# One weight product per rotated piece, and five fp4 pieces rounded by comparisons on VectorE and GpSimd and summed on TensorE

## What is computed

```python
# layer 0 attention: 16 heads of 32 for q, 8 for k and v, causal, soft cap 50
q, k = x @ Wq, x @ Wk                       # x: layernorm of the input
q = q * cos + rotate_half(q) * sin          # rotate_half: (-second half, first half) of each head's 32
k = k * cos + rotate_half(k) * sin
w = softmax(50 * tanh(q @ k.T / sqrt(32) / 50))   # masked
x = x + (w @ (x @ Wv)) @ Wo

# layer 0 feed-forward: weights rounded to fp4 in blocks of 32 along their input side
exp = floor(log2(max(max|w| over the block, 1e-30))) - 2
idx = digitize(|w / 2**exp|, [0.25, 0.75, 1.25, 1.75, 2.5, 3.5, 5.0])
w4  = sign(w) * [0, 0.5, 1, 1.5, 2, 3, 4, 6][idx] * 2**exp
```

## Time and profile before

| | |
|---|---|
| median of 3 runs | 1392.82 us (1390.68 to 1394.52) |
| the profiled execution | 1394.05 us, its span 1392.3 us |
| granted TensorE clock over the span | 0.953 |
| TensorE busy | 1239.9 us, 89% |
| VectorE busy | 817.3 us, 59% |
| ScalarE busy | 526.3 us, 38% |
| GpSimd busy | 329.8 us, 24% |

### The profile page before, as it was taken

One profiled execution on the slowest core, in us unless ns is written; L12 is line 12 of the kernel. 1 busy time (PEld: TensorE's weight loads), 2 busy tenths in 40 slices (PEclk: granted clock), 3 DMA queues, 4 the chain that ended last, 5 costly groups with the idle time before them and its releaser, 6 DMA issues. The chain is left out here.

```text
span 1392.3 us, 23432 instructions
## 1 busy us (share of the span) xinstructions
PE 1239.9 (89%) x9322; PEld 744.2 (53%) x9334; DVE 817.3 (59%) x2109; ACT 526.3 (38%) x967; POOL 329.8 (24%) x364
## 2 busy tenths in 40 slices
PE   5678779788999899899998998999999999994898
PEld 2246554456854544556664544555555555663455
DVE  2887767757687344768766766343111126777955
ACT  1019335563524433544444545111111114445453
POOL 0225502100003100245542221232222223450200
PEclk9688899998999999999999999999999999996999
DMA  9000000000040030000000000123232210000000
GB/s 384 1 0 3 1 1 2 0 1 1 1 197 2 10 112 1 1 2 3 3 2 1 2 2 1 52 75 95 80 106 80 84 37 1 2 3 0 1 1 31
DMA packets 13340, 48.02 MB, mean 34 GB/s; under 512 B 1688, under 2 KB 4888, under 8 KB 12464
## 3 DMA queue, kind: packets, MB, share of 16 engines
q1 hardware_dynamic: 13232, 46.53, 10.0%
HBM read 45.37 MB, written 1.15 MB: 33 GB/s over the span
## 5 line engine op out<-in xcount | busy, mean ns | idle before, releaser
L821 ACT ACTIVATE PT<-PS 128x384 f32<-128x384 f32 (+1 forms) x320 | 153.2, 531 | 189.3 <-PE PS L631 138.4
L1930 PE MATMUL PS<-HT,WA 128*128 128x512 f32 x448 | 201.5, 593 | 2.4 <-DVE MO L2008 2.0
L2008 DVE TENSOR_TENSOR MO<-PS,AO 128x512 f32<-128x512 f32 x56 | 38.7, 690 | 205.9 <-ACT AO L1998 205.8
L1930 PEld LDWEIGHTS PS<-HT,WA 128*128 128x128 f32 x448 | 84.7, 190 | 87.7 <-issue 82.9
L1998 ACT ACTIVATE AO<-PS 128x512 f32<-128x512 f32 x56 | 33.3, 597 | 247.9 <-PE PS L1930 247.9
L757 DVE CUSTOM_DVE_ANT_0 junk<-PS,TRI 128x128 bf16<-128x128 f32 (+1 forms) x384 | 112.6, 352 | 4.0 <-PE PS L612 0.2
L1938 PE MATMUL PS<-WA,HO 128*128 128x256 f32 x448 | 105.6, 378 | 0.0
L1938 PEld LDWEIGHTS PS<-WA,HO 128*128 128x128 f32 x448 | 84.5, 189 | 34.7 <-issue 24.9
L240 PE MATMUL PS<-identb 128*128 128x512 bf16 x388 | 99.2, 394 | 3.2 <-PEq L584 1.2
L2063 POOL TENSOR_TENSOR HO<-MO,GR 128x512 f32<-128x512 f32 x44 | 57.8, 1314 | 168.7 <-PE PS L1938 168.7
L612 PE MATMUL PS<-KS,QM 32*128 32x128 f32 (+1 forms) x768 | 86.7, 347 | 7.5 <-DVE QM L791 6.6
(11 more groups left out here) (323 smaller groups left out, 2412.8 us busy)
## 6 DMA issues: line engine op xcount, KB each, us to landing
WA<-w2f_in SPq DMA_DIRECT2D x28, 384.0 KB, 4.5
WA<-wl_in SPq DMA_DIRECT2D x1, 5137.0 KB, 16.0
GR<-gate_rows SPq DMA_DIRECT2D x20, 256.0 KB, 3.9
GB<-gate_rows SPq DMA_DIRECT2D x8, 512.0 KB, 7.4
WA<-wa_in SPq DMA_DIRECT2D x2, 1792.0 KB, 12.2
WB<-wb_in SPq DMA_DIRECT2D x1, 3208.0 KB, 18.4
WA<-wa_in SPq DMA_DIRECT2D x1, 2560.0 KB, 16.9
GR<-gate_rows SPq DMA_DIRECT2D x4, 448.0 KB, 4.0
```

Source lines behind the costliest of these rows:

```text
L821: act.activation(PT[:, g % 3, st_slot(k), 0:W], PS[:, st_bank(g, k), 0:W], ACT.Exp, scale=scale).then_inc(S["at_exp"], 1)
L1930: last = pe.matmul(PS[:, 2 * c + half, :], chunk(i, half)[:, k * P:(k + 1) * P], HT[:, k, c * CH:(c + 1) * CH], start=k == 0, stop=k == KD ...
```

## The change

It has four parts.

1. The swapped copies of the weights are gone, from the host's layout and from `a_in`. An item is a single product. VectorE exchanges the halves of each head by a stream shuffle from PSUM into `RS`, then multiplies the product by cos into `RC`. GpSimd multiplies `RS` by sin in place and adds. Four PSUM banks and four buffers now hold four items.
2. TensorE makes the product of v for tile n-2 right behind item n, in place of after all items. The context is turned behind the last item, in banks 4 and 5. GpSimd's wait for `b_in` is at the end of its block, and it waits for `const_in` first.
3. The five early pieces are rounded in another way. VectorE takes the largest of each block for all five pieces (items 1 to 3) and makes powers and inverses once on 80 columns. Per piece ScalarE makes the absolute value, VectorE scales it, and seven independent comparisons write 0 or a weight in bf16 into `IND`: four on VectorE, three on GpSimd. TensorE sums the seven by seven products with the bf16 identity (`identb`) into PSUM bank 6 or 7. VectorE joins sign and power (`SP`) and multiplies the sum by it. The pieces begin at the items 4, 5, 7, 8 and 10 (`turn`), TensorE sums two items later, or at the last item.
4. Beside the attention the same 51 steps now stand on 11 of the first 15 quads: none on the fourth quad of a batch, and none on the last.

```diff
-        work = [(w["q"], w["qp"], QT, j, c) for j in range(nq) for c in range(NCH)]
-        work += [(w["k"], w["kp"], KT, j, c) for j in range(2) for c in range(NCH)]
+        BUF = 4
+        work = [(w["q"], QT, j, c) for j in range(nq) for c in range(NCH)]
+        work += [(w["k"], KT, j, c) for j in range(2) for c in range(NCH)]
...
                 def _(pe):
-                    for n, (a, ap, _, j, c) in enumerate(work):
-                        if n >= 2:
-                            pe.wait_ge(S["rope_sin"], d["rope_sin"] + n - 1)
+                    for n, (a, _, j, c) in enumerate(work):
+                        if n >= 4:
+                            pe.wait_ge(S["rope_pair"], d["rope_pair"] + n - 3)
+                            pe.wait_ge(S["rope_cos"], d["rope_cos"] + n - 3)
+                        for k in range(KD):
+                            last = pe.matmul(PS[:, n % 4, :], a[:, k, j * P:(j + 1) * P],
+                                             HT[:, k, c * CH:(c + 1) * CH], start=k == 0, stop=k == KD - 1)
+                        last.then_inc(S["proj"], 1)
+                        t = n - 2
+                        if 0 <= t < TT:
...
+                        kernels["tensor"](pe, n, NW)
...
                 def _(dve):
+                        if n >= BUF:
+                            dve.wait_ge(S["rope_sum"], d["rope_sum"] + n - BUF + 1)
+                        dve.stream_shuffle(RS[:, n % BUF], ps, PAIR[hd]).then_inc(S["rope_pair"], 1)
+                        dve.tensor_tensor(wide(RC[:, n % BUF]), wide(ps), cos.to_broadcast([P, nchunk, T]),
+                                          ALU.mult).then_inc(S["rope_cos"], 1)
+                        kernels["vector"](dve, n, NW)
...
                 def _(pool):
+                    pool.wait_ge(S["const_in"], 16)
+                    for n, (_, dst, j, c) in enumerate(work):
+                        pool.wait_ge(S["rope_pair"], d["rope_pair"] + n + 1)
+                        pool.tensor_tensor(wide(RS[:, n % BUF]), wide(RS[:, n % BUF]), sin.to_broadcast([P, nchunk, T]),
+                                           ALU.mult).then_inc(S["rope_sin"], 1)
+                        pool.wait_ge(S["rope_sin"], d["rope_sin"] + n + 1)
+                        pool.wait_ge(S["rope_cos"], d["rope_cos"] + n + 1)
+                        pool.tensor_tensor(dst[:, j, c * CH:(c + 1) * CH], RC[:, n % BUF], RS[:, n % BUF], ALU.add).then_inc(S["rope_sum"], 1)
+                        kernels["beside"](pool, n, NW)
 
                     pool.wait_ge(S["b_in"], 64)
...
+        STEPS = [(5.0, 2.0), (3.5, 1.0), (2.5, 1.0), (1.75, 0.5), (1.25, 0.5), (0.75, 0.5), (0.25, 0.5)]
+        OWN = 4
...
+        def scaled(dve, m):
+            dve.wait_ge(S["q_sizes"], m + 1)
+            v = grp(at["scaled"][:, m % 4])
+            dve.tensor_tensor(v, v, wide(per(2, m)), ALU.mult).then_inc(S["q_scaled"], 1)
+        def sizes(act, m):
+            if m >= 4:
+                act.wait_ge(S["q_steps"], OWN * (m - 3))
+                act.wait_ge(S["q_steps_beside"], (len(STEPS) - OWN) * (m - 3))
+            act.activation(at["scaled"][:, m % 4], piece(m), ACT.Abs).then_inc(S["q_sizes"], 1)
+        def signed(dve, m):
+            if m >= 2:
+                dve.wait_ge(S["q_kept"], m - 1)
+            dve.scalar_tensor_tensor(u32(grp(at["signed"][:, m % 2])), u32(grp(piece(m))), 0x80000000, u32(wide(per(1, m))), ALU.bitwise_and,
+                                     ALU.bitwise_or).then_inc(S["q_signed"], 1)
+        def steps_of(eng, m, lo, hi, name):
+            eng.wait_ge(S["q_scaled"], m + 1)
+            if m >= 2:
+                eng.wait_ge(S["q_summed"], m - 1)
+            for j in range(lo, hi):
+                eng.tensor_scalar(at["steps"][:, m % 2, j, :], at["scaled"][:, m % 4], STEPS[j][0], STEPS[j][1], ALU.is_ge, ALU.mult).then_inc(S[name], 1)
+        def summed(pe, m):
+            for j in range(len(STEPS)):
+                last = pe.matmul(PS[:, 6 + m % 2, :], identb[:], at["steps"][:, m % 2, j, :], start=j == 0, stop=j == len(STEPS) - 1)
+            last.then_inc(S["q_summed"], 1)
+        def kept(dve, m):
+            dve.tensor_tensor(piece(m), PS[:, 6 + m % 2, :], at["signed"][:, m % 2], ALU.mult).then_inc(S["q_kept"], 1)
+        turn = {4: 0, 5: 1, 7: 2, 8: 3, 10: 4}
+        begun = {m: n for n, m in turn.items()}
...
         def beside_attention(dve, i, n):
-            lo, hi = (early * NS + (NP - early) * NS * min(j, n - 2) // (n - 2) for j in (i, i + 1))
+            lo, hi = (early * NS + (NP - early) * NS * min(j - j // 4, n - n // 4 - 1) // (n - n // 4 - 1) for j in (i, i + 1))
```

More of the change, by code:

```diff
@@ L892, in shifted_attention, with project @@
                 done[name] += k
-    def project(w, nq, hd, QT, KT, V, arrived=None, first=None, beside=None):
+    def project(w, nq, hd, QT, KT, V, kernels, arrived, first):
         cos = cst(f"cos{hd}", 1)
@@ L1126, in self_attention @@
         V = st.enter_context(nc.sbuf_tensor(f"V{layer}", [P, TT, D], F32))
-        project(w, nq, hd, QT, KT, V, arrived, first=masks, beside=beside[0])
+        project(w, nq, hd, QT, KT, V, beside[0], arrived, first=masks)
         copies, kernels = turn_kernels()
@@ new lines, in powers @@
+        def powers(dve):
+            a, b, c = (at["small"][:, j, :] for j in range(3))
+            dve.wait_ge(S["q_largest"], early)
+            dve.tensor_scalar(a, a, 1e-30, None, ALU.max).then_inc(S["q_powers"], 1)
+            dve.wait_ge(S["q_powers"], 1)
+            dve.tensor_scalar(u32(b), u32(a), 0x7F800000, None, ALU.bitwise_and).then_inc(S["q_powers"], 1)
+            dve.wait_ge(S["q_powers"], 2)
+            dve.tensor_scalar(b, b, 0.25, None, ALU.mult).then_inc(S["q_powers"], 1)
+            dve.wait_ge(S["q_powers"], 3)
+            dve.reciprocal(c, b).then_inc(S["q_powers"], 1)
+            dve.wait_ge(S["q_powers"], 4)
@@ new lines, in quantise_fp4, with beside_tensor, beside_vector @@
+        turn = {4: 0, 5: 1, 7: 2, 8: 3, 10: 4}
+        begun = {m: n for n, m in turn.items()}
+        def beside_tensor(pe, n, last):
+            for m in range(early):
+                if min(begun[m] + 2, last - 1) == n:
+                    summed(pe, m)
+        def beside_vector(dve, n, last):
+            if n in (1, 2, 3):
+                for m in range(2 * (n - 1), min(2 * n, early)):
+                    largest(dve, m)
+            if n == 3:
+                powers(dve)
+            if n in turn:
+                m = turn[n]
+                scaled(dve, m)
+                steps_of(dve, m, 0, OWN, "q_steps")
+            for m in range(early):
+                if begun[m] + 1 == n:
+                    signed(dve, m)
+                if begun[m] + 2 == n:
+                    kept(dve, m)
+            if n == last - 1:
+                kept(dve, early - 1)
@@ L2496, in gqa @@
         wk, wv = wk[:, cols], wv[:, cols]
-    if hd < 32:
-        return [blocks(a) for a in (wq, wk, wv, wo)]
-    return [blocks(a) for a in (wq, swapped(wq, hd, paired), wk, swapped(wk, hd, paired), wv, wo)]
+    return [blocks(a) for a in (wq, wk, wv, wo)]
 def layout(i):
```

137 lines of the change are left out of this document (66 added, 71 removed).

## The result

The changed kernel takes 1382.28 us (median of 6 runs, 1381.59 to 1383.8), the kernel before, run beside it, 1395.38 (1390.68 to 1400.27). The ratio is 0.9909, with an interval of 0.9893 to 0.9925: faster, by 13 us where 26 were forecast. The time lies above the range (1356 to 1379).

The account below looks back on a forecast made before the run. VectorE, busy for 61.85 of 67 us, was taken to bound the projection. The block ending 29 us earlier and the attention taking 3 more gave -26 us: 1368 from the profiled 1394.05, 1367 as median, range 1356 to 1379.

Parts of the forecast that it names:

- GpSimd's comparison: Projection: 15 comparisons new on GpSimd, priced at 0.77 us each from L2425, 11.6 us.
- GpSimd's lane: Projection: from 18.3 us, 42.1 of instructions, 6 of disturbance and 6.6 of waits, ending at 73.0.
- disturbance by VectorE: Projection: GpSimd loses 1.2 us per piece to VectorE's contested steps, 6 us in all.
- waits for a shuffle: Projection: GpSimd waits 1.65 us for the next item's shuffle at four of five pieces, 6.6 us.
- The last sum: End of projection: TensorE's last sum, 1.5 us or 3 at the low clock, hides behind GpSimd's last rotation.
- the whole walk: Projection: VectorE's and GpSimd's orders walked against each other; lanes end at 72.5 and 73.0, first attention product at 73.3.
- Rival B: Projection: GpSimd compares slower than it adds constants, 1.27 to 1.58 us each, +7 to +12, 1374 to 1379; 17%.
- rival E: Projection: slower than before, as GpSimd's comparison is too dear; decides at 2.5 us each, at 3.0 1400; 3%.
- The handing of work to GpSimd: Projection: three comparisons per piece on GpSimd; VectorE waits 3.9 us per piece in contested steps, 19 us.
- Rival C: Projection: TensorE at the low clock becomes the bound, 35 us of work become 70, 1382 us; 5%.
- rival F: Projection: VectorE and GpSimd exclude each other for whole instruction lengths, 1.32 in place of 1.05 us, 1370; 15%.
- The attention: Attention block: denser steps delay the first inversion 1.5 us and the second batch another 1.5; +3 us, between -2 and +6.

## Why the prediction was wrong in size and right in sign

**GpSimd's comparison** is the step that failed. It was priced at 0.77 us by a multiplication with an addition in the earlier trace rows, the nearest shape but another operation. The lane, term by term:

| GpSimd's lane, us | forecast | measured |
|---|---|---|
| first multiplication | 18.3 | 18.65 |
| 24 instructions with two inputs, undisturbed | 30.5 | 28.3 (12 x 1.09 + 12 x 1.27) |
| 15 comparisons, undisturbed | 11.6 | 28.8 (15 x 1.92) |
| disturbance by VectorE | 6 | 2.3 (0.5 + 0.6 + 1.2 of the three kinds) |
| waits for a shuffle | 6.6 | 1.8 |
| small gaps | 0 | 1.4 |
| end of its last rotation | 73.0 | 81.3 |
| then to the first attention product | 0.3 | 2.0 |

The comparisons give +17.2; the waits and disturbances shrink by 8.5, since VectorE now has time to be ahead; multiplication by sin in place is 2.2 cheaper in all, gaps and a later start cost 1.8: +8.3. The last sum, which was to hide behind the last rotation, adds 1.7. Near the assumed price the whole walk is right to 2.4 us, as the kernel with multiplication and addition shows, though there a disturbance that is too large by 2.8 makes up for waits that are too small by 2.7.

**Rival B** was the right mechanism, at 17%, but its own range ended at 1.58 us and 1379. The rows bounded it with instructions of other operations, and nothing in them excluded more; rival E even named the point (2.5 us) at which the price would make the kernel slower. With 1.92 in place of 0.77 the forecast's sum gives +17, 1384; the result is 1382.3. The upper bound was taken from the lengths of the nearest rows, although none of them was this comparison.

**The handing of work to GpSimd** was forecast to make VectorE wait for 19 us, and no kernel without it was among the rivals. With all seven on VectorE the block is 13 us shorter than in the changed kernel. It is 1.6 us shorter even than with GpSimd's instruction at 0.68 us (51.5 against 53.1 from GpSimd's first multiplication, the latter in one profile), so the handing over did not pay at the forecast's price either.

**TensorE** was not the bound: all five sums waited, for 1.5 to 7.7 us (forecast 2 to 4), and only the last lay on the path. Its mean clock was 0.76, below 0.8 as forecast; but in the earlier trace rows it is 0.78, so that sign could tell nothing. Rival C (1382) has the measured time by chance: the kernel with seven comparisons on VectorE has the same work on TensorE, and its attention starts at 68.9.

**The lock.** VectorE's steps beside GpSimd's comparisons (all but the fourth row) and beside its multiplications and additions (the fourth):

```profile
35.74 0.68 DVE L1238 TENSOR_TENSOR H<-H,SM 128x512 f32<-128x512 f32 x1
36.45 2.24 DVE L1261 TENSOR_SCALAR IND<-H 128x512 bf16<-128x512 f32 x4
...
43.32 0.68 DVE L1252 SCALAR_TENSOR_TENSOR SP<-WA,SM 128x512 uint32<-128x512 uint32 x1
...
47.47 4.34 DVE L1261 TENSOR_SCALAR IND<-H 128x512 bf16<-128x512 f32 x4
```

GpSimd compares without a pause from 32.98 to 39.4 and from 41.86 to 47.7. In those times a scaling and a sign, both with two inputs, take VectorE 0.68 us, as alone; the comparisons around the sign take GpSimd 5.81, three times 1.92; and four comparisons of VectorE take 2.24, 0.8 more than alone (3 x 0.34 + 0.42), since two of them take 0.83 and 0.82. From 47.6 to 52.9 GpSimd multiplies and adds, and the same four take 4.34; a scaling at 30.54, beside a multiplication and an addition, takes 1.23. So rival F (the pair excludes each other for the whole lengths) falls where GpSimd compares. The Trainium skill ("SBUF — State Buffer", Who interferes with whom) has an instruction of VectorE with two inputs from SBUF contend with any of GpSimd's that reads there; the sign's row shows none of it beside a comparison.

**The attention** took +3.0, as forecast, and the forecast's mechanism is in it. The forecast counted about two more steps ahead of the first inversion, where its own shares of 4.6 and 3.6 a quad give three. The inversions came 1.0, 2.4, 2.9 and 3.0 us later counted from the block's start (forecast 1.5 and 3), and TensorE waited 4.56 us at the first, where it had 2.96 at that place before. But the +3 was the difference to a block whose clock history had changed too: with the old spread behind the new projection the block takes 76.6 to 79.6. So the agreement is in part luck. And the cross attention's 2.3 us, through the clock, were not in the sum, nor the 1.9 of the rest, which one profile each can't tell from scatter (it takes 1143.0 to 1147.3 in the thirteen profiles). In all the spread costs 6 to 7 us in the three comparisons of medians, in place of 3.

## What to carry to other kernels

An operation has a price on each engine: take it from a row with the same operation, and where none exists, bound it by factors and not by the neighbours' lengths. Before handing an instruction of 0.41 us to a second engine, ask whether the first one has time (here it had), since the lane that gets it and the waits that tie the two cost more. Steps put beside other work belong behind the instructions for which the others wait, and longer waits cost more than themselves through TensorE's clock: here waits shorter by 2.8 us made a block shorter by 5.3.

## What was not expected of the hardware

- On GpSimd, for 128x512 f32: multiplication with addition 0.68 us, a comparison 1.49, a comparison with a multiplication 1.92, with bf16 or f32 output alike. On VectorE the last takes 0.41.
- A multiplication of two inputs in place, with the broadcast cos or sin as the second, takes GpSimd 1.09 us; the addition to another tile 1.27.
- GpSimd's work disturbs VectorE by its operation. Beside a comparison VectorE's steps with two inputs take 0.68 us as alone, and four of its comparisons 2.24 in place of 1.44; beside multiplications and additions the same four take 4.34, and a step with two inputs 1.23.
- After waits of TensorE of the same length, 2.96 us, 16 products took 0.86 us in some blocks and 1.50 in others; after those of 4.5 us, 1.43 or more each time.
